# Second attention of a decoder layer: last batch's norms and row turns, and the second key turn, moved behind the turned probabilities and the value matmuls

## The reference

```python
Q = (q @ Wq.T + bq).reshape(bs, sl, H, HD)      # q: the layer's x; H = 16, HD = 32
K = (k @ Wk.T + bk).reshape(bs, sl, H, HD)      # k, v: the context
V = (v @ Wv.T + bv).reshape(bs, sl, H, HD)
score = jnp.einsum('bshd,bsgd->bshg', Q, K)
weight = jax.nn.softmax(score, axis=-1)
attn = jnp.einsum('bshg,bsgd->bshd', weight, V).reshape(bs, sl, nf)
return attn @ Wo.T + bo
# in the layer: x = layernorm(x + self_attention(x)); x = layernorm(x + this(x, ctx)); x = layernorm(x + experts(x))
```

## Time and profile before

| what | us |
|---|---|
| median of three runs | 2038.64 |
| the profiled execution | 2038.83 |
| its span, first to last instruction | 2036.8 |
| TensorE busy | 1910.0 |
| VectorE busy | 1095.2 |
| ScalarE busy | 669.0 |
| GpSimd busy | 259.2 |
| second attention, within the span | 363 to 668 |

### The profile page before, as it was taken

One profiled execution on the slowest core, in us unless ns is written; L12 is line 12 of the kernel. 1 busy time (PEld: TensorE's weight loads), 2 busy tenths in 40 slices (PEclk: granted clock), 3 DMA queues, 4 the chain that ended last, 5 costly groups with the idle time before them and its releaser, 6 DMA issues.

```text
span 2036.8 us, 33248 instructions
## 1 busy us (share of the span) xinstructions
PE 1910.0 (94%) x12912; PEld 1513.5 (74%) x12912; DVE 1095.2 (54%) x1780; ACT 669.0 (33%) x1461; POOL 259.2 (13%) x239
## 2 busy tenths in 40 slices
PE   5999995799996899999999999999999999999997
PEld 5777774678875577777777777777777777777775
DVE  4555554567674445563555463554645554635565
ACT  5556654211220333342232332332322322323321
POOL 2335334223231000000000000000000000000000
PEclk9999998899997899999999999999999999999999
DMA  2011012100000202021020030020210300200011
GB/s 88 22 31 31 21 31 90 32 21 10 21 0 1 88 1 76 23 68 35 13 82 13 7 87 6 13 80 6 64 29 12 81 12 6 87 6 12 7 47 42
DMA packets 38910, 71.50 MB, mean 35 GB/s; under 512 B 7232, under 2 KB 15552, under 8 KB 38080
## 3 DMA queue, kind: packets, MB, share of 16 engines
q1 hardware_dynamic: 38848, 70.63, 11.3%
HBM read 64.85 MB, written 5.77 MB: 35 GB/s over the span
## 4 chain that ended last, share of the span: by engine, by line
PE 64%; issue 1%; DVE 1%; ACT 1%; POOLq 0%; POOL 0%; DVEq 0%
PE pair L1661 11%; PE pair L1663 11%; PE pair L1662 11%; PE y_ps L1661 3%; PE y_ps L1662 3%; PE qa_ps L1661 3%; PE y_ps L1663 3%; PE qa_ps L1662 3%; PE qa_ps L1663 2%; PE pair L1783 2%; PE pair L1784 2%; PE qd_ps L1830 1%; PE pair L1745 1%; PE qd_ps L1831 1%; PE qd_ps L1662 1%
## 5 line engine op out<-in xcount | busy, mean ns | idle before, releaser
L1661 PE MATMUL pair<-XH,GUH 128*128 128x512 f32 (+1 forms) x960 | 375.9, 392 | 0.0
L1663 PE MATMUL pair<-XH,GUL 128*128 128x512 f32 (+1 forms) x960 | 375.6, 391 | 0.0
L1662 PE MATMUL pair<-XL,GUH 128*128 128x512 f32 (+1 forms) x960 | 374.6, 390 | 0.0
L1575 DVE TENSOR_TENSOR h<-pair,sg 128x512 f32<-128x512 f32 (+1 forms) x120 | 82.8, 690 | 426.3 <-ACT sg L1363 426.1
L1363 ACT ACTIVATE sg<-pair 128x512 f32<-128x512 f32 (+1 forms) x120 | 71.7, 597 | 477.2 <-PE pair L1784 382.1
L1663 PEld LDWEIGHTS pair<-XH,GUL 128*128 128x128 f32 (+1 forms) x960 | 171.7, 179 | 47.7
L1662 PEld LDWEIGHTS pair<-XL,GUH 128*128 128x128 f32 (+1 forms) x960 | 171.8, 179 | 47.4
L1661 PEld LDWEIGHTS pair<-XH,GUH 128*128 128x128 f32 (+1 forms) x960 | 171.6, 179 | 47.1
L1265 POOL TENSOR_TENSOR qb_raw<-qb_raw,qb_scale 128x704 f32<-128x704 f32 x8 | 13.7, 1710 | 1066.4 <-DMA qb_scale<-in_gu_scale 1066.4
L1275 ACT ACTIVATE XH<-xe 128x512 fp32r<-128x512 f32 x128 | 78.8, 633 | 179.0 <-DVE xe L1597 179.0
L262 ACT ACTIVATE p<-s_ps,nm 128x128 f32<-128x128 f32 (+1 forms) x256 | 103.8, 428 | 76.5 <-DVE nm L345 76.5
(11 more groups left out here) (295 smaller groups left out, 4042.3 us busy)
## 6 DMA issues: line engine op xcount, KB each, us to landing
gu_raw<-in_gu SPq DMA_DIRECT2D x20, 512.0 KB, 4.2
wrep<-soft_f SPq DMA_DIRECT2D x64, 128.0 KB
dw_raw<-in_dw SPq DMA_DIRECT2D x10, 512.0 KB, 3.9
xT_raw<-in_xT SPq DMA_DIRECT2D x8, 512.0 KB, 3.8
x_raw<-in_x SPq DMA_DIRECT2D x8, 512.0 KB, 3.6
c_raw<-in_cT SPq DMA_DIRECT2D x8, 512.0 KB, 3.8
out<-xtok SPq DMA_DIRECT2D x4, 1024.0 KB, 4.2
gu_raw<-in_gu SPq DMA_DIRECT2D x10, 384.0 KB, 3.1
```

The lines of the kernel that those rows point to most:

```text
L1575: nc.vector.tensor_tensor(h[0:M, b, :], pair[b][1][0:M, :], sg[0:M, b, :], ALU.mult).then_inc(h_rdy, 1)
L1661: mm(out, wh, xh, start=first, stop=False)
L1662: mm(out, wh, xl, start=False, stop=False)
L1663: return mm(out, wl, xh, start=False, stop=last)
```

## The change

The calls in three of the `batch` functions stand in another order; no instruction is added or removed. VectorE: the reciprocals before the first key turn; the second key turn and the norms of batch b - 1 behind `probs_turned`. TensorE: projection 3 straight after 2, then `values`, then row turn 0, projection 4, row turn 1, projection 5. ScalarE: the two `features_out` behind `o_high`.

```diff
@@ ScalarE @@
             def batch(b, first, last):
                 exps(b, 0)
                 exps(b, 1)
-                if not first:
-                    if ahead(b, 1):
-                        values_out(b + 1, 0)
-                    features_out(b - 1, 0)
-                    if ahead(b, 1):
-                        values_out(b + 1, 1)
-                    features_out(b - 1, 1)
-                else:
+                if ahead(b, 1):
                     values_out(b + 1, 0)
                     values_out(b + 1, 1)
                 if ahead(b, 2):
                     context_high(b + 2)
                 o_high(b, 0)
                 o_high(b, 1)
+                if not first:
+                    features_out(b - 1, 0)
+                    features_out(b - 1, 1)
                 if ahead(b, 2):
                     x_high(b + 2)
@@ VectorE @@
                 less_maxima(b, 0)
                 less_maxima(b, 1)
+                reciprocals(b, 0)
+                reciprocals(b, 1)
                 if ahead(b, 1):
                     keys_turned(b + 1, 0)
-                reciprocals(b, 0)
-                reciprocals(b, 1)
+                probs_turned(b, 0)
+                probs_turned(b, 1)
+                if ahead(b, 1):
+                    keys_turned(b + 1, 1)
                 if not first:
                     norm_out(b - 1, 0)
                     norm_out(b - 1, 1)
-                if ahead(b, 1):
-                    keys_turned(b + 1, 1)
-                probs_turned(b, 0)
-                probs_turned(b, 1)
@@ TensorE @@
                 scores(b)
                 if not last:
-                    project(b + 1, 0)
-                    project(b + 1, 1)
-                    project(b + 1, 2)
+                    for n in range(4):
+                        project(b + 1, n)
+                values(b)
                 if not first:
                     turn_rows(b - 1, 0)
                 if not last:
-                    project(b + 1, 3)
+                    project(b + 1, 4)
                 if not first:
                     turn_rows(b - 1, 1)
-                values(b)
                 if not last:
-                    project(b + 1, 4)
                     project(b + 1, 5)
                 outputs(b, 0, not last)
```

## The result

| | us |
|---|---|
| kernel before, median of 6 | 2039.12 |
| changed kernel, median of 6 (2018.50 to 2028.85) | 2025.57 |
| ratio | 0.9928, 95% interval 0.991 to 0.9946 |
| a second series: changed, median of 6 (2022.90 to 2027.67) | 2025.80 |
| its ratio | 0.9937, 95% interval 0.9922 to 0.9952 |

Faster, by 0.6 to 0.7%. The ratios compare all executions of a series; they aren't the quotient of the two medians, which is 0.9934 in the first. So one series alone can't tell the forecast of 2027.0 from this. All executions together can: 65 of the kernel before and 12 of the changed one, those whose granted clock is on record, have means of 2039.0 and 2025.1.

A forecast was written before the change was run, and what follows sets the result against it. TensorE, busy 94% of the span, was taken as the bound, so only its waits could pay. Gains of 10.0 + 0.9 + 0.8 = 11.7 us from 2038.83 gave a forecast of 2027.0 us, range 2024.5 to 2033.0.

The forecast's parts named there:

- The wait goes, and what ends last there is TensorE's own work: Inner batches: TensorE reaches the value matmuls 0.3 us after the turned probabilities (pb), so its wait there vanishes.
- Gain 1.67 us: Inner batches 1 to 6: TensorE's idle time counted start to start, 1.67 us each, 10.0 us for six.
- I take 0.9: Batch 0: value matmuls start earlier because pb ends earlier; 0.9 us gained, bounds 0 and 1.0.
- pb against the loading of code: Batch 0: whether the 0.87 us before the value matmuls is a wait for pb or code loading, which would gain nothing.
- I take 0.8: Last batch: output matmuls start earlier, part of 1.3 us given back to the second row turn; 0.8 us, bounds 0.3 and 1.3.
- the stalls inside it stay: Last batch: value matmuls start at 643.2 and end at 650.7, the stalls within them unchanged.
- 11.7 us: Whole kernel: total gain, 10.0 for the inner batches, 0.9 for the first and 0.8 for the last.
- I keep -2 to +3 for it: TensorE's clock: two half-clock spells may each grow or go by some 2 us; -2 to +3 allowed, outside the sum.
- The range runs from 2024.5: Whole kernel time: 2024.5 to 2033.0 us, the low end from the forecast's own clock allowance, rounded.
- Rival C: TensorE's clock falls in every inner batch, up to 3.2 us each; 7.5 us slower, time 2046.3; chance 0.03.
- A measurement of this kernel can tell about 0.2%: Whole kernel: a time difference of about 0.2%, 4.1 us, can be told from no change.

The follow-up runs named there:

- e3: Changed kernel with VectorE's list as before the change, so only TensorE's and ScalarE's part; median 2042.42 us, ratio 1.002 to the kernel before.
- e7: Changed kernel with VectorE's norms put back ahead of the turned probabilities; median 2037.69 us, ratio 0.9989 to the kernel before.
- e8: Changed kernel with VectorE's second key turn put back ahead of the turned probabilities; median 2035.83 us, ratio 0.9985 to the kernel before.
- e2: Changed kernel with TensorE's and ScalarE's lists as before the change, so only VectorE's part; median 2068.36 us, ratio 1.0147 to the kernel before.
- e5: Changed kernel with batches 0 and 7 back in the old order on all three engines; median 2028.73 us, ratio 0.9952 to the kernel before.
- e4: Changed kernel with norms ahead of the maxima and, in the last batch, row turns and copies ahead of the values; median 2027.23 us, ratio 0.995.

## Why the prediction was right, and where not

- "The wait goes, and what ends last there is TensorE's own work": shown, by the rows above, and by e3 and e7, in which the wait stays and with it the time, and by e8, which moves only VectorE's work and lets the wait back in. That both halves are needed (e2, e3) was not said, but follows from the same chain.
- "Gain 1.67 us" per inner batch: 1.46 to 1.47. The start-to-start count took the steps to last as long in the new order as in the old. Values to first row turn take 4.18 us (508.13 - 503.95) where 4.05 stood, and each row turn with the projection behind it some 0.05 more. Six batches give 8.8, not 10.0.
- Batch 0, "I take 0.9": 0.95, and e5 and e8 have the gap back. The choice for pb against the loading of code was right.
- Last batch, "I take 0.8": 0.3 for the start of the outputs, 0.9 up to the experts, of which the clock has a part. The values came sooner than forecast (1.5 us for 1.3), and longer stalls inside them (0.5 us) took more than that back, where the prediction had "the stalls inside it stay".
- Sum "11.7 us": 8.8 + 0.95 + 0.3 to 0.9 is 10.1 to 10.7 by order alone; 10.6 in the profiles from stage start to stage end; 11.6 at equal half-clock time. The mechanism and the size of the order's part stand; about 1 us between the sum of the rows and the line is not explained, and that the line meets the forecast's 11.7 so closely is in part luck, with the inner term 1.2 us too high.
- The step that failed is the clock: "I keep -2 to +3 for it", with no term in the sum, and "The range runs from 2024.5". In its place, TensorE's half-clock time fell by 8 us and brought an estimated 2.4 us on top. With the low end only 2.5 us below the forecast, that was enough for the 2024.0 that the first ratio gives to lie outside; by half a microsecond, so that which side of the end it fell on was chance (the 13.9 us of all executions give 2024.7, just inside), but the missing 2 us were not. The low end had even been rounded down: 2026.9 with -2 and +3 is 2024.9 to 2029.9. The bound was on two spells seen in one profile; about half of an execution's half-clock time lies outside the stage (40.7 of 79.6 us in that profile), and executions of one kernel differ by 9 us (2033 to 2042 before). Why the changed kernel is granted the full clock more often stays open.
- The same step read the spread between executions as no more than an unknown. The Trainium skill's sentence on runs of one kernel that differ ("TensorE: Matmul & The Clock Gate", Part 1: The HAM clock gate) is borne out here as to the spread: 2018.5 to 2028.9 over six executions of the changed kernel, whose mean granted clocks were 0.986 and 0.980 in those two. The reason that the page gives is not something that these runs show.
- Rival C (the clock falls in every inner batch) is not what happened, 1.00 over 456 to 616; but e2 and e3 show that it exists in this kernel, with 4.4 and 2.3 us of waiting in each inner batch.
- "A measurement of this kernel can tell about 0.2%": the intervals here are 0.1 to 0.2% wide to either side. Right.

## What to carry to other kernels

In a hand-ordered pipeline the wait belongs to the whole chain between two engines: here moving work out of the chain on one engine paid only once the other engine's list no longer asked for that work in between (e2, e3), so look at both lists before moving either. Before moving an operation forward, look up when its own input is ready; an instruction that never waited can start to wait once what stood ahead of it is gone (e8). And when a gain is worked out from one profiled execution, put beside the sum how far the granted clock of single executions moves the time, the same width to both sides.

## What the runs showed of the hardware

- Two copies of 1.04 us on the path cost nothing that shows in the mean (2039.2 and 2025.0 against 2039.0 and 2025.1), while TensorE's half-clock time fell by 5 to 6 us. One microsecond granted at half clock went with 0.29 us of time on average, where dense matmuls alone would lose half. Much of it lies in idle time: in the profile of before, TensorE was idle for 22.0 of the 27.3 us of the spell around the stage's start (339.2 to 366.5).
- The granted clock fell in every one of batches 2 to 6 with 4.4 us (e2) and with 2.31 us of waiting (e3) beside the small matmuls, and in none of them with 1.44 (before), 1.80 (e7) or 1.03 (e8).
- VectorE's norm of one half took 0.54 and 0.55 us with GpSimd idle (e4), but 1.39 and 1.27 us beside GpSimd's key bias (changed kernel and before); both norms together took 1.86 us before and 1.84 in the changed kernel, where the second one took 0.54. The two divides of GpSimd went from 2.24 to 2.06 us when no norm ran beside them. The Trainium skill ("SBUF — State Buffer", SBUF: two separate sides) has an exclusive lock between the two engines; the trace agrees that they hold each other up, but doesn't show that one blocks the other wholly.
